# Scan decays moved from PSUM to SBUF, the freed banks given to a shared ring, pieces placed anew

## Chip, core and metric

One NeuronCore of one Trainium2 chip runs the whole program. The metric is device time of that core in microseconds (us); one execution was also taken with the hardware profiler. The engines are TensorE (PE in the profile, with its weight loads as PEld), VectorE (DVE), ScalarE (ACT), GpSimd (POOL) and SyncE (SP), which only issues transfers here.

## What is computed

x is 4 sequences of 1024 tokens with 256 channels. After a layer norm two things are made of it: a routed feed-forward stage (eight experts, one per token), and eight state-space (Mamba) layers with 512 inner channels and 16 states. The result is x + s * silu(ffn). Almost all of the time is in the eight layers:

```
xin, z = split(x @ W_in.T);  u = silu(causal_conv(xin, 4 taps) + b)
x_dbl  = u @ W_x.T  ->  dt_raw (16), B (16), C (16)
delta  = softplus(dt_raw @ W_dt.T + b_dt);  A = -exp(A_log)
h_t[c, n] = h_{t-1}[c, n] * exp(delta_t[c] * A[c, n]) + (delta_t[c] * u_t[c]) * B_t[n]
y_t[c] = sum_n h_t[c, n] * C_t[n] + u_t[c] * D[c]
x = x + (y * silu(z)) @ W_out.T
```

## The kernel before

`program` calls `experts`, then `mamba`, then `finish`. The change touches `mamba` alone and the tables of numbers that it reads.

**Units and tiles.** `mamba` works in 64 units: 8 layers times 4 sequences times 2 halves of 512 time steps (T = 512). A unit has 64 tiles (TILES = 16 states x 4 blocks of 128 channels); tile k is state n = k // 4, block j = k % 4. For each tile:
- ScalarE makes the decay exp(delta * A), 128x512 fp32 (`exponent`, L907), into `ps_d`, two banks of PSUM, two tiles ahead of the scan;
- GpSimd makes the drive, du times a row of B repeated over the partitions, both in SBUF, into one of eight buffers in SBUF (`drive`, L875); it may be up to eight tiles ahead;
- VectorE runs the recurrence over the 512 steps as one scan instruction (L1069), whose two tensor inputs are the decay in PSUM and the drive in SBUF. In the second half of a sequence (h = 1) the start value comes from `carry`, which GpSimd keeps (L861).

After the four tiles of a state, TensorE transposes the state, four matmuls for each quarter t of the time (`turn_state`, L1225), into a ring in PSUM, `ps_r`; ScalarE multiplies by C and writes `prod` in SBUF (`weigh`, L914); TensorE turns `prod` back and adds it up in `ps_y`, four banks (`turn_back`, L1232). The eight banks of PSUM are so: `ps_d` two, `ps_r` two, `ps_y` four.

**Software pipeline.** In the slots (n, t) of a unit U the engines also do pieces of other units: the end of U-1 (`gate` L1167, `out_proj` L1313, `add_x` L1173), the late half of U+1 (x and dt projections, softplus L1127 to L1137, `make_du` L1117, z), and the early half of U+2 (the marks and the running minimum that masks overflowed sequences, `mark_over` L1078/L1080, `keep_alive` L1091, `mask_x` L846 on GpSimd, `in_x`, and the convolution). Three of the four blocks are convolved on VectorE, four steps each (L1104, then L1108 three times, all in SBUF), one on TensorE (L1284). A program order written out by hand says in which slot each piece is: the tables `RING_AT`, `SILU_AT`, `EXP_AT`, `LN_AT`, `MARK_AT`, `ALIVE_AT`, `ADD_AT`, `GATE_AT`, `SKIPY_AT`, `SOFT_AT`, `CONV_AT`, `DU_AT`, `HALO_AT`, `XM_AT`. Slots from (16, 0) on mean the next unit's slot (n - 16, t). All of an engine's work runs in this order, and waits are on counting semaphores.

**The ring.** Each thing that TensorE hands to ScalarE or VectorE through `ps_r` is an item; `item_place` gives it bank (count of items so far) % 2, and `place_free` makes TensorE wait until the reader of the item two before it is done.

Of the kernel before, what the change touches and what calls it, by code (L numbers as in the profile page):

```python
# [25 lines left out]
F32 = mybir.dt.float32  # L26
# [45 lines left out]
XD = RANK + 2 * STATES  # L72
BREP = 4
DRIVE = 8
CARRY_LAG = 9
TABLE = "natural_log_exp_and_others"


RING_AT = {"CNT": (3, 0), "O0": (4, 1), "O1": (5, 3), "XD": (4, 2), "BC": (7, 3), "DT0": (6, 0), "DT1": (6, 2), "DT2": (8, 0),
           "DT3": (9, 2), "Z0": (10, 1), "Z1": (11, 3), "Z2": (14, 1), "Z3": (15, 0), "X0": (5, 0), "X1": (8, 3),  # L80
           "X2": (10, 3), "X3": (14, 2), "C3": (17, 0)}
SILU_AT, EXP_AT, LN_AT = (4, 2), [(7, 0), (10, 1)], [(8, 3), (11, 3)]
MARK_AT, ALIVE_AT, ADD_AT = [(2, 1), (2, 2)], (3, 1), [(4, 3), (6, 1)]
PE_CONV, DVE_CONV = [3], [0, 1, 2]
GATE_AT, SKIPY_AT = [(1, 1), (1, 2), (1, 2), (1, 2)], [(1, 1), (1, 3), (1, 3), (1, 3)]
SOFT_AT = [(7, 3), (8, 3), (9, 3), (10, 2), (10, 3), (11, 3), (14, 2), (14, 3)]
CONV_AT = [(5, 2), (5, 2), (6, 0), (6, 2), (9, 2), (10, 1), (12, 2), (12, 3), (15, 1), (17, 0), (17, 3), (19, 0)]
DU_AT = [(14, 3), (14, 3)]
HALO_AT, XM_AT = (3, 2), (5, 1)
CONV_ITEMS = [f"C{j}" for j in PE_CONV]  # L90
CV = CB - len(PE_CONV)
READ_AT = {name: divmod(CB * n + t + 1, CB) for name, (n, t) in RING_AT.items()}
# [509 lines left out]
def item_place(U, h, kind, name):  # L602

    i = ITEMS[kind].index(name)
    if isinstance(items_before(U, kind)[0], int):
        return (items_before(U, kind)[0] + i) % 2
    return (h * len(ITEMS["mid"]) + PRE_ALL + i) % 2


def item_ready(U, kind, name):  # L610
# [22 lines left out]

def place_free(U, kind, name):

    i = ITEMS[kind].index(name)
    if kind == "pre0" and i < 2:
        return None
    act, vec = reads(U, kind, i - 1)
    if i >= 2 and ITEMS[kind][i - 2] in VEC_ITEMS:  # L640
        return "vec", vec
    return "act", act


def mamba(nc, w_in, w_x, w_dt, w_out, w_skip, w_conv, a_log, par, xres, ident, alive_dram, bc_dram, rate_dram):

    with ExitStack() as ctx:
# [13 lines left out]
        ones_time = sb("ones_time", [1, T], BF16)  # L661
        zeros = sb("zeros", [P, 1])

        over = sb("over_mark", [P, 2, DB, T], BF16)
        alive = [sb(f"alive{h}", [P, T]) for h in range(2)]
        xm = [sb(f"xm{h}", [P, DB, T]) for h in range(2)]
        low = sb("low", [P, 2, T])
        xpad = sb("xpad", [P, CB, TAPS - 1 + T])
# [4 lines left out]
        xdbl = sb("xdbl", [P, T])  # L673
        bcT = [sb(f"bcT{h}", [P, TC, XD]) for h in range(2)]
        soft = sb("soft", [P, CB, T])
        rates = soft[:, 0, 0:LAYERS * NA]
        relu = sb("relu", [P, CB, T])
        gated = relu
# [2 lines left out]

        brep = sb("brep", [P, BREP, T])
        drive = sb("drive", [P, DRIVE, T])
        state = [sb(f"state{k}", [P, CB, T]) for k in range(2)]
        carry = sb("carry", [P, STATES, CB])
        prod = sb("prod", [P, TC, INNER])

        ps_d = ctx.enter_context(nc.psum_tensor("ps_d", [P, 2, T], F32))
        ps_r = ctx.enter_context(nc.psum_tensor("ps_r2", [P, 2, 512], F32))
        ps_y = ctx.enter_context(nc.psum_tensor("ps_y", [P, CB, T], F32))  # L690

        par_in, par_exp, par_set, par_out = sem("par_in"), sem("par_exp"), sem("par_set"), sem("par_out")
# [15 lines left out]
        def is_first(U):  # L708
            return isinstance(U, int) and U == 0
# [13 lines left out]
        def _(sp):  # L723
# [22 lines left out]
            def store_alive(U, kind, G):  # L746
                h = G % 2
                sp.wait_ge(ring_vec, item_read(U, kind, "CNT"))
                c = (G // HALVES % BATCH) * SEQ + h * T
                sp.dma_start(alive_dram[:, c:c + T], alive[h][0:1, :]).then_inc(alive_out[h], 16)  # L750

            def store_bc(U, kind, F):
                sp.wait_ge(ring_act, item_read(U, kind, "XD"))
# [81 lines left out]
        def _(pool):  # L835
# [5 lines left out]
            def mask_x(U, kind, G, h, it):  # L841
                pool.wait_ge(ring_vec, item_read(U, kind, "CNT"))
                if not (isinstance(G, int) and G < 2):

                    pool.wait_ge(ring_ready, items_before(U, kind)[0])
                nc.gpsimd.tensor_tensor(xm[h][:], xres[:, :, bass.ds((it % BATCH) * SEQ + h * T, T)],  # L846
                                        alive[h][:].unsqueeze(1).to_broadcast([P, DB, T]), ALU.mult).then_inc(xm_set, 1)

            def halo(U, kind, F, h):

# [45 lines left out]
        def _(act):  # L896
            def exponent(U, h, k):

                n, j = divmod(k, CB)
                if k in (0, CB // 2):  # L900
                    act.wait_ge(delta_set, 2 * U + k // 2 + 1)
                if not (is_first(U) and k < 2):
                    act.wait_ge(scanned, TILES * U + k - 1)
                a = j * STATES + n
                if k == 0:
                    act.wait_ge(cur_in[h], loads_of(U, h))
                nc.scalar.activation(ps_d[:, k % 2, :], delta[h][:, j, :], ACT.Exp, scale=cur[h][:, a:a + 1]).then_inc(decay_set, 1)  # L907

            def weigh(U, h, kind, item, V, n, t):

# [97 lines left out]
            def unit(U, h, it, kind):  # L1008
                for n in range(STATES):
                    for t in range(TC):  # L1010
                        k = CB * n + t + 2
                        if k < TILES:
                            exponent(U, h, k)
                        elif kind != "last":
                            exponent(U + 1, 1 - h, k - TILES)
                        if (n, t) == SILU_AT:
                            if kind != "last":
                                silu_u(U, kind, U + 1)
                            silu_z(U, h, kind)
                            nc.scalar.preload_act_table_set(TABLE)  # L1020
                        if kind != "last":
                            late(U, h, kind, U + 1, 1 - h, n, t)
                        if kind in ("first", "mid"):
                            early(U, h, kind, U + 2, n, t)
                        if n:
                            weigh(U, h, kind, ("S", n - 1, t), U, n - 1, t)
                        elif kind != "first":
                            weigh(U, h, kind, ("S", "prev", t), U - 1, STATES - 1, t)
# [13 lines left out]
            for n in range(STATES):  # L1042
                for t in range(TC):
                    early(0, 0, "pre1", 1, n, t)
            exponent(0, 0, 0)
            exponent(0, 0, 1)
            units(act, unit)
            for t in range(TC):
                weigh(UNITS, 0, "end", ("S", "prev", t), UNITS - 1, STATES - 1, t)
# [2 lines left out]
        def _(dve):  # L1052
            def scan(U, h, it, kind, n, j):
                k = CB * n + j
                dve.wait_ge(decay_set, TILES * U + k + 1)
                dve.wait_ge(drive_set, TILES * U + k + 1)
                if j == 0 and not (is_first(U) and n < 2):

                    if n >= 2:
                        dve.wait_ge(ring_ready, item_ready(U, kind, ("S", n - 2, TC - 1)))  # L1060
                    elif n == 1:
                        dve.wait_ge(ring_ready, item_ready(U, kind, ("S", "prev", TC - 1)))
                    else:
                        dve.wait_ge(ring_ready, items_before(U, kind)[0])
                    if h == 0 and n >= 2:
                        dve.wait_ge(carried, STATES * it + n - 1)
                    if h == 1:
                        dve.wait_ge(carried, STATES * it + min(STATES - 1 + n, STATES))
                nc.vector.tensor_tensor_scan(state[n % 2][:, j, :], ps_d[:, k % 2, :], drive[:, k % DRIVE, :],  # L1069
                                             carry[:, n, j:j + 1] if h == 1 else 0.0, ALU.mult, ALU.add).then_inc(scanned, 1)  # L1070

            def mark_over(U, kind, F, h, it, side):

                if kind != "pre0":
                    dve.wait_ge(ring_vec, items_before(U, kind)[1])
                xs = xres[:, :, bass.ds((it % BATCH) * SEQ + h * T, T)]
                if side == 0:
                    nc.vector.tensor_scalar(over[:, 0], xs, LIMIT, None, ALU.is_gt).then_inc(over_set, 1)  # L1078
                else:
                    nc.vector.tensor_scalar(over[:, 1], xs, -LIMIT, None, ALU.is_lt).then_inc(over_set, 1)  # L1080

            def keep_alive(U, h, kind, F, hf):

                dve.wait_ge(ring_ready, item_ready(U, kind, "CNT"))
                if not (isinstance(F, int) and F < 2):
                    dve.wait_ge(xm_set, F - 1)
                    if isinstance(F, int):
                        dve.wait_ge(alive_out[hf], 16 * (F // 2))
                    else:
                        dve.wait_ge(alive_out[hf], 8 * (F - hf))  # L1090
                nc.vector.tensor_tensor_scan(alive[hf][:], ps_r[:, item_place(U, h, kind, "CNT"), :], zeros[:, 0:1].to_broadcast([P, T]),  # L1091
                                             alive[0][:, T - 1:T] if hf == 1 else 1.0, ALU.min, ALU.max).then_inc(ring_vec, 1)

            def conv(copied, G, h, j, k):

# [436 lines left out]
```

## Time and profile before

| | us |
|---|---|
| median of 3 runs | 7806.82 |
| lowest, highest | 7770.17, 7848.79 |
| the profiled execution, its own time | 7796.76 |
| its span in the trace | 7795.0 |
| mean granted TensorE clock | 0.991 |

The span runs from the first instruction to the end of the last; busy times of the engines overlap. A number behind "idle before" in a row is the time in which that engine did nothing just before the instructions of the row, with what ended it.

### The profile page before, as it was taken

What the parts mean: (1) busy time and instruction counts of PE and PEld (TensorE: products, weight loads), DVE (VectorE), ACT (ScalarE), POOL (GpSimd) and SP (SyncE); (2) the same over time, 40 slices, a digit from 0 to 9 for tenths busy, and PEclk for the clock granted to TensorE, in tenths of its full rate; (3) what the DMA queues carried; (4) which work ended last, traced back from release to release, by engine and by line L of the source; (5) the groups of instructions that cost most, each with busy time, mean ns of one, the idle gap of its engine ahead of it and who ended that gap; (6) DMA issues with size and microseconds to landing.
All of it is one profiled execution on the core that took longest, in us unless ns stands there. A gap on an engine that the chain in (4) does not pass through costs nothing. (4 is left out here: it accounts for less than half of the span.)

```text
span 7795.0 us, 144019 instructions
## 1 busy us (share of the span) xinstructions
PE 6935.7 (89%) x39999; PEld 4781.3 (61%) x40063; DVE 6645.2 (85%) x6512; ACT 6436.9 (83%) x10314; POOL 5919.1 (76%) x4917
## 2 busy tenths in 40 slices
PE   6978999888999999999899999999998899999887
PEld 4646666666666666666666666666666666666665
DVE  3259888988988898889888988988898898889888
ACT  2248888888888888888888888888888888888887
POOL 2137888787888888888878887888888778888875
PEclk9989999999999999999999999999999999999998
DMA  4111111111111111111111111111111111111112
GB/s 160 33 40 37 39 40 47 42 38 38 42 45 43 39 39 43 46 40 40 39 46 44 40 38 42 45 42 39 39 47 42 38 39 42 45 43 39 39 38 90
DMA packets 222613, 352.40 MB, mean 45 GB/s; under 512 B 43856, under 2 KB 78448, under 8 KB 221712
## 3 DMA queue, kind: packets, MB, share of 16 engines
q1 hardware_dynamic: 218048, 332.70, 14.5%
q0 software_dynamic: 3792, 10.38, 0.4%
q8 instruction: 365, 5.98, 0.3%
q14 instruction: 408, 3.34, 0.1%
HBM read 325.00 MB, written 17.98 MB: 44 GB/s over the span
## 5 line engine op out<-in xcount | busy, mean ns | idle before, releaser
L875 POOL TENSOR_TENSOR drive<-du,brep 128x512 f32<-128x512 f32 x4096 | 5495.8, 1371 | 715.0 <-DVE du L1117 360.0
L907 ACT ACTIVATE ps_d<-delta,cur 128x512 f32<-128x512 f32 x4096 | 2844.6, 695 | 447.3 <-DVE state L1069 428.1
L914 ACT ACTIVATE prod<-ps_r,bcT 128x512 f32<-128x512 f32 x4096 | 2807.1, 685 | 240.0 <-PE ps_r L1225 235.4
L1225 PE MATMUL ps_r<-ident,state 128*128 128x128 f32 x16384 | 2552.5, 279 | 326.1 <-ACT prod L914 180.5
L1069 DVE TENSOR_TENSOR_SCAN state<-ps_d,carry,drive 128x512 f32<-128x512 f32 x2048 | 2503.2, 1264 | 308.9 <-PE ps_r L1225 274.8
L1069 DVE TENSOR_TENSOR_SCAN state<-ps_d,drive 128x512 f32<-128x512 f32 x2048 | 2390.7, 1207 | 300.8 <-PE ps_r L1225 239.6
L1232 PE MATMUL ps_y<-ident,prod 128*128 128x128 f32 x16384 | 2467.1, 275 | 25.9 <-ACT prod L914 25.9
L1232 PEld LDWEIGHTS ps_y<-ident,prod 128*128 128x128 f32 x16384 | 1928.7, 142 | 663.5 <-issue 511.7
L1225 PEld LDWEIGHTS ps_r<-ident,state 128*128 128x128 f32 x16384 | 1834.7, 141 | 773.4 <-ACT prod L914 497.3
L1273 PE MATMUL ps_r<-xm,w_inz_sb 128*128 128x512 f32 x1024 | 509.1, 620 | 89.3 <-ACT prod L914 89.3
L1265 PE MATMUL ps_r<-xm,w_inx_sb 128*128 128x512 f32 x1024 | 509.1, 621 | 25.4 <-ACT prod L914 13.9
L1313 PE MATMUL ps_r<-relu,w_out_sb 128*128 128x512 f32 x1024 | 474.2, 606 | 58.7 <-ACT prod L914 56.0
L1108 DVE SCALAR_TENSOR_TENSOR xc<-xpad,taps,xc 128x512 f32<-128x512 f32 x576 | 505.4, 877 | 4.2 <-issue 1.5
L861 POOL COPY carry<-state 128x4 f32<-128x4 f32 x512 | 226.3, 442 | 232.2 <-DVE state L1069 230.3
L1306 PE MATMUL ps_r<-xdbl,w_dt_sb 16*128 16x512 f32 x512 | 290.1, 647 | 90.2 <-DVE xres L1173 47.2
L1313 PEld LDWEIGHTS ps_r<-relu,w_out_sb 128*128 128x128 f32 x1024 | 184.7, 190 | 273.3 <-issue 217.7
L1273 PEld LDWEIGHTS ps_r<-xm,w_inz_sb 128*128 128x128 f32 x1024 | 174.4, 190 | 270.1 <-ACT prod L914 134.5
L1265 PEld LDWEIGHTS ps_r<-xm,w_inx_sb 128*128 128x128 f32 x1024 | 175.9, 191 | 196.0 <-issue 154.5
L534 ACT ACTIVATE hid<-ps_t,b_sb 128x128 f32<-128x128 f32 x312 | 84.8, 382 | 227.5 <-PE ps_t L495 227.5
L1292 PE MATMUL ps_r<-u,w_x_sb 128*48 128x512 f32 x512 | 233.7, 600 | 34.1 <-ACT u L942 34.1
L462 POOL DMA_INDIRECT ys_dram<-yb,row x39 | 37.4, 959 | 296.8 <-DVE yb L554 296.8
L1243 PE MATMUL ps_y<-u,skip 128*128 128x512 f32 x512 | 241.3, 594 | 4.6 <-DVE relu L1167 4.5
(148 smaller groups left out, 4586.5 us busy)
## 6 DMA issues: line engine op xcount, KB each, us to landing
brep<-bc_dram SPq DMA_DIRECT2D x1024, 256.0 KB, 3.2
w_sb<-w SPq DMA_DIRECT2D x8, 1024.0 KB
w_all<-w SPq DMA_DIRECT2D x8, 1024.0 KB, 11.4
xb<-xs_dram SPq DMA_DIRECT2D x39, 128.5 KB, 2.0
w_all<-x SPq DMA_DIRECT2D x4, 1024.0 KB, 9.0
w_inx_sb<-w_in SPq DMA_DIRECT2D x8, 512.0 KB, 4.0
w_inz_sb<-w_in SPq DMA_DIRECT2D x8, 512.0 KB, 4.4
w_out_sb<-w_out SPq DMA_DIRECT2D x8, 512.0 KB, 4.3
```

What stands on the lines that cost most here:

```text
L875: nc.gpsimd.tensor_tensor(drive[:, k % DRIVE, :], du[:, j, :], brep[:, n % BREP, :], ALU.mult).then_inc(drive_set, 1)
L907: nc.scalar.activation(ps_d[:, k % 2, :], delta[h][:, j, :], ACT.Exp, scale=cur[h][:, a:a + 1]).then_inc(decay_set, 1)
L914: nc.scalar.activation(prod[:, t, :], ps_r[:, item_place(U, h, kind, item), :], ACT.Copy, scale=bcT[(h + 1) % 2 if item[1] == "prev" else ...
L1069: nc.vector.tensor_tensor_scan(state[n % 2][:, j, :], ps_d[:, k % 2, :], drive[:, k % DRIVE, :], carry[:, n, j:j + 1] if h == 1 else 0.0, ...
L1108: step = nc.vector.scalar_tensor_tensor(xc[:, j, :], xpad[:, j, tap:tap + T], w, xc[:, j, :], ALU.mult, ALU.add)
L1225: last = nc.tensor.transpose(out[:, j * P:(j + 1) * P], state[n % 2][:, j, t * P:(t + 1) * P], ident[:])
L1232: last = nc.tensor.matmul(ps_y[:, j, t * P:(t + 1) * P], prod[:, t, j * P:(j + 1) * P], ident[:], start=False, stop=True, is_transpose=Tru ...
L1243: last = nc.tensor.matmul(ps_y[:, j, :], skip[:, j, :], u[:, j, :], start=True, stop=True, skip_group_check=True)
L1265: last = nc.tensor.matmul(out, w_inx_sb[:, k, j * P:(j + 1) * P], xm[h][:, k, :], start=(k == 0), stop=(k == DB - 1))
L1273: last = nc.tensor.matmul(out, w_inz_sb[:, k, j * P:(j + 1) * P], xm[hf][:, k, :], start=(k == 0), stop=(k == DB - 1))
L1306: nc.tensor.matmul(out, w_dt_sb[:, j * P:(j + 1) * P], xdbl[0:RANK, :], start=True, stop=True).then_inc(ring_ready, 1)
L1313: last = nc.tensor.matmul(out, w_out_sb[:, j, k * P:(k + 1) * P], gated[:, j, :], start=(j == 0), stop=(j == CB - 1))
```

## The change

1. The decays go to `decay`, four buffers of 128x512 in SBUF, and ScalarE is four tiles ahead of the scan in place of two (LEAD = 4). The scan then has both of its tensor inputs in SBUF.
2. The two banks of `ps_d` join the ring: `ps_r` has four banks (RING = 4), and `place_free` looks four items back.
3. To find room in SBUF, the overflow marks `over` lie in the third and fourth quarter of `soft` (so `mark_over` also waits on `delta_set`), and the two `alive` buffers become one (`keep_alive` waits for the mask before and for the store before).
4. All tables of slots have new values.

```diff
+LEAD = 4
+RING = 4
-RING_AT = {"CNT": (3, 0), "O0": (4, 1), "O1": (5, 3), "XD": (4, 2), "BC": (7, 3), "DT0": (6, 0), "DT1": (6, 2), "DT2": (8, 0),
-           "DT3": (9, 2), "Z0": (10, 1), "Z1": (11, 3), "Z2": (14, 1), "Z3": (15, 0), "X0": (5, 0), "X1": (8, 3),
-           "X2": (10, 3), "X3": (14, 2), "C3": (17, 0)}
-SILU_AT, EXP_AT, LN_AT = (4, 2), [(7, 0), (10, 1)], [(8, 3), (11, 3)]
-MARK_AT, ALIVE_AT, ADD_AT = [(2, 1), (2, 2)], (3, 1), [(4, 3), (6, 1)]
+RING_AT = {"CNT": (0, 3), "O0": (3, 3), "O1": (4, 1), "XD": (7, 3), "BC": (10, 1), "DT0": (8, 3), "DT1": (9, 2),
+           "DT2": (10, 3), "DT3": (12, 3), "Z0": (13, 1), "Z1": (13, 3), "Z2": (14, 1), "Z3": (15, 2), "X0": (2, 3),
+           "X1": (6, 0), "X2": (9, 1), "X3": (15, 1), "C3": (16, 2)}
+SILU_AT, EXP_AT, LN_AT = (4, 0), [(10, 1), (13, 1)], [(11, 2), (14, 1)]
+MARK_AT, ALIVE_AT, ADD_AT = [(0, 2), (0, 2)], (0, 3), [(4, 1), (5, 0)]
-GATE_AT, SKIPY_AT = [(1, 1), (1, 2), (1, 2), (1, 2)], [(1, 1), (1, 3), (1, 3), (1, 3)]
-SOFT_AT = [(7, 3), (8, 3), (9, 3), (10, 2), (10, 3), (11, 3), (14, 2), (14, 3)]
-CONV_AT = [(5, 2), (5, 2), (6, 0), (6, 2), (9, 2), (10, 1), (12, 2), (12, 3), (15, 1), (17, 0), (17, 3), (19, 0)]
-DU_AT = [(14, 3), (14, 3)]
-HALO_AT, XM_AT = (3, 2), (5, 1)
+GATE_AT, SKIPY_AT = [(1, 0), (1, 0), (1, 0), (1, 1)], [(1, 0), (1, 0), (1, 2), (1, 2)]
+SOFT_AT = [(11, 0), (11, 3), (12, 1), (14, 1), (14, 1), (14, 1), (14, 3), (15, 0)]
+CONV_AT = [(4, 1), (4, 3), (6, 1), (8, 3), (9, 0), (9, 1), (10, 0), (10, 3), (12, 3), (13, 0), (14, 2), (16, 1)]
+DU_AT = [(15, 0), (15, 3)]
+HALO_AT, XM_AT = (1, 0), (2, 2)
...
 def item_place(U, h, kind, name):
...
-        return (items_before(U, kind)[0] + i) % 2
-    return (h * len(ITEMS["mid"]) + PRE_ALL + i) % 2
+        return (items_before(U, kind)[0] + i) % RING
+    return (h * len(ITEMS["mid"]) + PRE_ALL + i) % RING
...
 def place_free(U, kind, name):
-    i = ITEMS[kind].index(name)
-    if kind == "pre0" and i < 2:
+    i = ITEMS[kind].index(name) - RING
+    if kind == "pre0" and i < 0:
         return None
-    act, vec = reads(U, kind, i - 1)
-    if i >= 2 and ITEMS[kind][i - 2] in VEC_ITEMS:
-        return "vec", vec
-    return "act", act
+    if i < 0:
+        before = {"pre1": "pre0", "first": "pre1", "mid": "mid", "near": "mid", "last": "near", "end": "last"}[kind]
+        assert not any(x in VEC_ITEMS for x in ITEMS[before][i:])
+        return "act", items_before(U, kind)[2] + i + 1
+    act, vec = reads(U, kind, i + 1)
+    return ("vec", vec) if ITEMS[kind][i] in VEC_ITEMS else ("act", act)
...
-        over = sb("over_mark", [P, 2, DB, T], BF16)
-        alive = [sb(f"alive{h}", [P, T]) for h in range(2)]
+        alive = sb("alive", [P, T])
...
+        over = soft[:, 2:4, :].rearrange("p a t -> p (a t)").bitcast(BF16).rearrange("p (s k t) -> p s k t", s=2, k=DB)
...
+        decay = sb("decay", [P, LEAD, T])
...
-        ps_d = ctx.enter_context(nc.psum_tensor("ps_d", [P, 2, T], F32))
-        ps_r = ctx.enter_context(nc.psum_tensor("ps_r2", [P, 2, 512], F32))
+        ps_r = ctx.enter_context(nc.psum_tensor("ps_r2", [P, RING, 512], F32))
...
             def exponent(U, h, k):
-                if not (is_first(U) and k < 2):
-                    act.wait_ge(scanned, TILES * U + k - 1)
+                if not (is_first(U) and k < LEAD):
+                    act.wait_ge(scanned, TILES * U + k + 1 - LEAD)
...
-                nc.scalar.activation(ps_d[:, k % 2, :], delta[h][:, j, :], ACT.Exp, scale=cur[h][:, a:a + 1]).then_inc(decay_set, 1)
+                nc.scalar.activation(decay[:, k % LEAD, :], delta[h][:, j, :], ACT.Exp, scale=cur[h][:, a:a + 1]).then_inc(decay_set, 1)
...
             def scan(U, h, it, kind, n, j):
-                nc.vector.tensor_tensor_scan(state[n % 2][:, j, :], ps_d[:, k % 2, :], drive[:, k % DRIVE, :],
+                nc.vector.tensor_tensor_scan(state[n % 2][:, j, :], decay[:, k % LEAD, :], drive[:, k % DRIVE, :],
                                              carry[:, n, j:j + 1] if h == 1 else 0.0, ALU.mult, ALU.add).then_inc(scanned, 1)
...
             def mark_over(U, kind, F, h, it, side):
                 if kind != "pre0":
                     dve.wait_ge(ring_vec, items_before(U, kind)[1])
+                    dve.wait_ge(delta_set, 2 if kind == "pre1" else 2 * U + 2)
...
             def keep_alive(U, h, kind, F, hf):
-                if not (isinstance(F, int) and F < 2):
-                    dve.wait_ge(xm_set, F - 1)
+                if not is_first(F):
+                    dve.wait_ge(xm_set, F)
                     if isinstance(F, int):
-                        dve.wait_ge(alive_out[hf], 16 * (F // 2))
+                        dve.wait_ge(alive_out[1 - hf], 16 * ((F + hf) // 2))
                     else:
-                        dve.wait_ge(alive_out[hf], 8 * (F - hf))
-                nc.vector.tensor_tensor_scan(alive[hf][:], ps_r[:, item_place(U, h, kind, "CNT"), :], zeros[:, 0:1].to_broadcast([P, T]),
-                                             alive[0][:, T - 1:T] if hf == 1 else 1.0, ALU.min, ALU.max).then_inc(ring_vec, 1)
+                        dve.wait_ge(alive_out[1 - hf], 8 * (F + hf))
+                nc.vector.tensor_tensor_scan(alive[:], ps_r[:, item_place(U, h, kind, "CNT"), :], zeros[:, 0:1].to_broadcast([P, T]),
+                                             alive[:, T - 1:T] if hf == 1 else 1.0, ALU.min, ALU.max).then_inc(ring_vec, 1)
```

## Rows read from the trace of the kernel before

**Rows 1.** Table of stretches, one steady and one before the units: busy us of each engine.

```profile
2100.00:2800.00 700.00, 634.09 (x3734) 436.45 (x3739) 628.35 (x595) 609.87 (x962) 568.78 (x461) 1.00 0.15 42
450.00:500.00 50.00, 35.71 (x67) 12.56 (x66) 22.93 (x26) 19.59 (x26) 2.53 (x2) 0.80 0.09 31
```

**Rows 2.** The page's costliest groups: busy us, mean ns of one, idle before and releaser.

```profile
L875 POOL TENSOR_TENSOR drive<-du,brep 128x512 f32<-128x512 f32 x4096 | 5495.8, 1371 | 715.0 <-DVE du L1117 360.0
L907 ACT ACTIVATE ps_d<-delta,cur 128x512 f32<-128x512 f32 x4096 | 2844.6, 695 | 447.3 <-DVE state L1069 428.1
L914 ACT ACTIVATE prod<-ps_r,bcT 128x512 f32<-128x512 f32 x4096 | 2807.1, 685 | 240.0 <-PE ps_r L1225 235.4
L1069 DVE TENSOR_TENSOR_SCAN state<-ps_d,carry,drive 128x512 f32<-128x512 f32 x2048 | 2503.2, 1264 | 308.9 <-PE ps_r L1225 274.8
L1069 DVE TENSOR_TENSOR_SCAN state<-ps_d,drive 128x512 f32<-128x512 f32 x2048 | 2390.7, 1207 | 300.8 <-PE ps_r L1225 239.6
```

**Rows 3.** Table of waits of the whole span: us in total, times, longest.

```profile
DVE state L1069 <- PE ps_r L1225: 514.4, 263, 9.4
PE ps_r L1225 <- ACT prod L914: 180.5, 326, 2.2
```

**Rows 4.** The scans' line: durations min/median/max, first and last start.

```profile
L1069 DVE TENSOR_TENSOR_SCAN state<-ps_d,drive x2048: 1189/1207/1226, 519.1 to 7640.6; 128x512 f32<-128x512 f32 x187
L1069 DVE TENSOR_TENSOR_SCAN state<-ps_d,carry,drive x2048: 1248/1259/1285, 632.0 to 7727.5; 128x512 f32<-128x512 f32 x187
```

**Rows 5.** Timeline, GpSimd drives beside scans: start us, us, instructions merged.

```profile
4119.25 4.97 POOL L875 TENSOR_TENSOR drive<-du,brep 128x512 f32<-128x512 f32 x4
...
4137.17 5.71 DVE L1069 TENSOR_TENSOR_SCAN state<-ps_d,drive 128x512 f32<-128x512 f32 x5
...
4117.90 8.32 DVE L1069 TENSOR_TENSOR_SCAN state<-ps_d,carry,drive 128x512 f32<-128x512 f32 x7
```

**Rows 6.** Timeline, one convolution step on VectorE between two drives on GpSimd.

```profile
4114.32 1.28 POOL L875 TENSOR_TENSOR drive<-du,brep 128x512 f32<-128x512 f32 x1
...
4115.27 0.87 DVE L1108 SCALAR_TENSOR_TENSOR xc<-xpad,taps,xc 128x512 f32<-128x512 f32 x1
...
4115.55 1.73 POOL L875 TENSOR_TENSOR drive<-du,brep 128x512 f32<-128x512 f32 x1
```

**Rows 7.** Timeline, VectorE pieces of 1024 columns beside a drive on GpSimd.

```profile
4109.45 1.27 POOL L875 TENSOR_TENSOR drive<-du,brep 128x512 f32<-128x512 f32 x1
...
4110.54 1.26 DVE L1130 TENSOR_TENSOR low<-soft,low 128x1024 f32<-128x1024 f32 x1
...
4130.71 1.21 DVE L1117 TENSOR_TENSOR du<-delta,u 128x1024 f32<-128x1024 f32 x1
...
4130.95 2.10 POOL L875 TENSOR_TENSOR drive<-du,brep 128x512 f32<-128x512 f32 x1 [6.73 <-DVE du L1117]
```

**Rows 8.** Lines with their durations over the whole span, min/median/max ns.

```profile
L875 POOL TENSOR_TENSOR drive<-du,brep x4096: 1251/1275/2301, 505.4 to 7720.6; 128x512 f32<-128x512 f32 x196
L1108 DVE SCALAR_TENSOR_TENSOR xc<-xpad,taps,xc x576: 716/755/5796, 460.0 to 7553.5; 128x512 f32<-128x512 f32 x192
L1104 DVE TENSOR_SCALAR xc<-xpad,taps x192: 514/547/1923, 459.5 to 7528.2; 128x512 f32<-128x512 f32 x192
L1134 DVE TENSOR_TENSOR low<-low,delta x128: 1191/1196/1226, 486.3 to 7631.6; 128x1024 f32<-128x1024 f32 x128
L1127 DVE TENSOR_SCALAR low<-soft x128: 660/668/1623, 483.6 to 7611.7; 128x1024 f32<-128x1024 f32 x128
L1078 DVE TENSOR_SCALAR over_mark<-xres x64: 659/661/686, 447.4 to 7432.0; 128x1024 bf16 x60, 128x1024 bf16<-128x1024 f32 x4
L846 POOL TENSOR_TENSOR xm<-xres,alive x64: 2337/2362/2379, 452.6 to 7446.5; 128x1024 f32<-128x1024 f32 x64
```

**Rows 9.** Groups by line and form, VectorE: one input in PSUM, or both in SBUF.

```profile
L1452 DVE TENSOR_TENSOR clean<-clean,valid 128x1024 f32<-128x1024 f32 x8 | 9.8, 1225 | 0.3
L1463 DVE TENSOR_TENSOR gate<-gate,ps_f 128x1024 f32<-128x1024 f32 x8 | 9.7, 1214 | 0.0
L1167 DVE TENSOR_TENSOR relu<-ps_y,zs 128x512 f32<-128x512 f32 x256 | 160.9, 667 | 5.1 <-PE ps_y L1232 5.1
```

**Rows 10.** Groups by line: TensorE's convolution, and ScalarE's silus and table loads.

```profile
L1284 PE MATMUL ps_r<-xpad,conv_w 128*128 128x512 f32 x512 | 232.0, 595 | 0.8 <-ACT xpad L920 0.8
L942 ACT ACTIVATE u<-xc 128x2048 f32<-128x2048 f32 x64 | 122.7, 1917 | 0.7
L942 ACT ACT_TABLE_LOAD x64 | 82.1, 1283 | 1.2
```

More of the change, by code:

```diff
@@ L74 @@
 DRIVE = 8
+LEAD = 4
+RING = 4
 CARRY_LAG = 9
 TABLE = "natural_log_exp_and_others"
-RING_AT = {"CNT": (3, 0), "O0": (4, 1), "O1": (5, 3), "XD": (4, 2), "BC": (7, 3), "DT0": (6, 0), "DT1": (6, 2), "DT2": (8, 0),
-           "DT3": (9, 2), "Z0": (10, 1), "Z1": (11, 3), "Z2": (14, 1), "Z3": (15, 0), "X0": (5, 0), "X1": (8, 3),
-           "X2": (10, 3), "X3": (14, 2), "C3": (17, 0)}
-SILU_AT, EXP_AT, LN_AT = (4, 2), [(7, 0), (10, 1)], [(8, 3), (11, 3)]
-MARK_AT, ALIVE_AT, ADD_AT = [(2, 1), (2, 2)], (3, 1), [(4, 3), (6, 1)]
-PE_CONV, DVE_CONV = [3], [0, 1, 2]
-GATE_AT, SKIPY_AT = [(1, 1), (1, 2), (1, 2), (1, 2)], [(1, 1), (1, 3), (1, 3), (1, 3)]
-SOFT_AT = [(7, 3), (8, 3), (9, 3), (10, 2), (10, 3), (11, 3), (14, 2), (14, 3)]
-CONV_AT = [(5, 2), (5, 2), (6, 0), (6, 2), (9, 2), (10, 1), (12, 2), (12, 3), (15, 1), (17, 0), (17, 3), (19, 0)]
-DU_AT = [(14, 3), (14, 3)]
-HALO_AT, XM_AT = (3, 2), (5, 1)
+RING_AT = {"CNT": (0, 3), "O0": (3, 3), "O1": (4, 1), "XD": (7, 3), "BC": (10, 1), "DT0": (8, 3), "DT1": (9, 2),
[3 more added lines that the diff above has]
+MARK_AT, ALIVE_AT, ADD_AT = [(0, 2), (0, 2)], (0, 3), [(4, 1), (5, 0)]
+PE_CONV, DVE_CONV = [3], [0, 1, 2]
+GATE_AT, SKIPY_AT = [(1, 0), (1, 0), (1, 0), (1, 1)], [(1, 0), (1, 0), (1, 2), (1, 2)]
+LOW_AT = [(3, 3), (8, 0)]
+SOFT_AT = [(11, 0), (11, 3), (12, 1), (14, 1), (14, 1), (14, 1), (14, 3), (15, 0)]
+CONV_AT = [(4, 1), (4, 3), (6, 1), (8, 3), (9, 0), (9, 1), (10, 0), (10, 3), (12, 3), (13, 0), (14, 2), (16, 1)]
+DU_AT = [(15, 0), (15, 3)]
+HALO_AT, XM_AT = (1, 0), (2, 2)
 CONV_ITEMS = [f"C{j}" for j in PE_CONV]
@@ L749, in store_alive @@
                 c = (G // HALVES % BATCH) * SEQ + h * T
-                sp.dma_start(alive_dram[:, c:c + T], alive[h][0:1, :]).then_inc(alive_out[h], 16)
+                sp.dma_start(alive_dram[:, c:c + T], alive[0:1, :]).then_inc(alive_out[h], 16)
             def store_bc(U, kind, F):
@@ L846, in mask_x @@
                 nc.gpsimd.tensor_tensor(xm[h][:], xres[:, :, bass.ds((it % BATCH) * SEQ + h * T, T)],
-                                        alive[h][:].unsqueeze(1).to_broadcast([P, DB, T]), ALU.mult).then_inc(xm_set, 1)
+                                        alive[:].unsqueeze(1).to_broadcast([P, DB, T]), ALU.mult).then_inc(xm_set, 1)
             def halo(U, kind, F, h):
@@ L1010, in unit @@
                     for t in range(TC):
-                        k = CB * n + t + 2
+                        k = CB * n + t + LEAD
                         if k < TILES:
@@ L1044, in _ @@
                     early(0, 0, "pre1", 1, n, t)
-            exponent(0, 0, 0)
-            exponent(0, 0, 1)
+            for k in range(LEAD):
+                exponent(0, 0, k)
             units(act, unit)
```

## The prediction

> **What bounds the kernel now.** I read first the table of stretches: in a steady 700 us TensorE is busy 634, VectorE 628, ScalarE 610 and GpSimd 569 us, at full clock [rows 1]. Four engines are within 10% of each other, so no engine alone is the bound; what each waits for must be read next. The scans run from 519.1 to 7727.5 + 1.3 = 7728.8 us [rows 4]; that is 7209.7 us for 64 units, **112.65 us for a unit**, 1.76 us for each of its 64 tiles. 519.1 us lie ahead and 7795.0 - 7728.8 = 66.2 us behind. VectorE is at work for 628/700 of a unit, 101.1 us, and idle for 11.5. The table of waits says for what: 514.4 us, 8.0 a unit, are scans that wait for TensorE's transposes, at most 9.4 us at once [rows 3], and TensorE in its turn waits 180.5 us for ScalarE to empty the ring of two banks. ScalarE sits idle for 428.1 us because decays may be made only two tiles ahead of the scans [rows 2]. These are the stalls that the change aims at: the two short queues between TensorE, ScalarE and VectorE.
>
> **What VectorE and GpSimd do to each other.** This is the view that decides, since the change alters where a scan reads. GpSimd's drive (two inputs in SBUF) takes 1.27 us as a rule but up to 2.30 [rows 8]. The timeline shows when. Beside scans four drives in a row take 4.97 us, one every (4.97 - 1.27)/3 = 1.23, and five scans 5.71, one every (5.71 - 1.22)/4 = 1.12 (1.18 with a carry, from 8.32 for seven) [rows 5]: neither feels the other. A scan has one tensor input in PSUM. Now a convolution step, whose two tensor inputs are both in SBUF: the drive ahead of it ends at 4114.32 + 1.28 = 4115.60; the step, begun at 4115.27, ends at 4116.14, 0.54 after that drive, and takes 0.87 in place of the 0.72 that it takes alone; the next drive, begun at 4115.55, ends at 4117.28, 1.14 after the step, and takes 1.73 [rows 6]. So they don't overlap at all: each does its data part only when the other is done. The same with 1024 columns: a softplus piece ends 4111.80 - 4110.72 = 1.08 after the drive that was running, and the drive that begins during a du piece ends 4133.05 - 4131.92 = 1.13 after it and takes 2.10 [rows 7]. VectorE's pieces with one input in PSUM (the gate, 667 ns in the mean [rows 9]) show no such stretch. I read it as a path into SBUF that VectorE's second SBUF input and GpSimd's reads share, held by one instruction at a time: a drive holds it for 1.13 us, a VectorE instruction of 1024 fp32 columns for 1.08, one of 512 for 0.54.
>
> The Trainium skill says this as a rule ("SBUF — State Buffer", Who interferes with whom): a VectorE instruction with two SBUF inputs contends with a GpSimd instruction that reads SBUF, and the loser is blocked for the whole instruction. It names no scan, and no row here has a long scan with two SBUF inputs; by that rule every one of the 4096 would take turns with a drive, which is my forecast.
>
> **The change, part by part.**
>
> *Decays in SBUF.* All scans now have two tensor inputs in SBUF. Their own duration should stay: two inputs in SBUF take 1225 ns and one of them in PSUM 1214, same shape [rows 9]. But what a scan holds must be bounded. It takes 1207 ns for 512 steps, as a 1024-column piece does (1196) [rows 4, 8], so it moves an element every second cycle for as long; the nearest row for its hold is that piece, 1.08 us. Above, its own start-to-start, 1.12, or 1.18 with a carry [rows 5]; below nothing, if a scan doesn't read through that path (rival one). The 57 ns that a carry adds (1264 against 1207 [rows 2]) may lie in the hold or not: half of the units have it, and I take half of it in them, 0.015 in the mean, and as much again for the hand-over. A drive: 1.13, above it its start-to-start, 1.23 [rows 5]. So a tile costs 1.08 + 0.03 + 1.13 = **2.24 us** (bounds 2.21 and 1.16 + 1.23 = 2.39), in place of 1.76, and 64 tiles cost **143.4 us** (141.4 to 153.0). Being ahead doesn't help, since both instructions have to pass for each tile.
>
> *What else passes there in a unit*: nine convolution steps of 0.54, 4.9; three first steps, alone 0.51 with some 0.17 outside the hold (0.72 - 0.54, as in the other steps), 1.0; six softplus pieces of two inputs and two du pieces, 8 x 1.08 = 8.6; two of one input, faster by half (0.66), and two marks (0.66), 4 x 0.5 = 2.0; GpSimd's mask, 2.36 - 0.14 = 2.2; eight carry copies of four columns, 0.4 together [rows 6 to 8]. Whether the one-input forms hold the path is less sure; nothing else changes if not. Sum **19.1** (17 if not).
>
> *Lead of four, ring of four.* They take away waits of VectorE, TensorE and ScalarE: 8.0 + 2.8 + 6.7 us a unit. These engines have 101 us of work or less in a unit [rows 1], which now lasts over 160, so the waits were going to be hidden by the slower tile anyway: **zero** gained. The same holds for what the decay costs ScalarE in SBUF rather than PSUM: even 0.1 us more, 6 us a unit, has 50 us of cover. The silus at (4, 0) keep ScalarE from decays for 1.92 and 1.89 us with two table loads of 1.28, 6.4 us [rows 10]; four tiles ahead are 4 x 2.24 = 9.0, so no scan waits for them; with the lead of two it would be 1.9 us a unit.
>
> The Trainium skill has a rule that speaks for the change here ("VectorE: DVE Perf Modes", the TRN2 errata): VectorE's fixed cost is 120 cycles from PSUM against 58 in SBUF, by which 4096 scans would be an estimated 260 us cheaper. The rows of one shape don't show it (1214 against 1225), and with a path that is full a shorter fixed part buys nothing.
>
> *Pieces placed anew.* Their count is the same, so the sum above stays; the question is where the path is idle because both engines wait. Three places at the start of a unit: (a) du comes at (15, 0) and (15, 3), where before both pieces came at (14, 3). GpSimd may make only drives 0 and 1 of the next unit until scan 63 and du are done; scans 61 to 63 use the path meanwhile, nothing lost; bound 2 x 1.13. (b) GpSimd waits at (1, 0) for the last convolution step and TensorE's item C3 (for the halo) with everything queued behind it, drives 5 on; it has five drives done by then. (c) The gates are at (1, 0), behind scan 4, and wait for all of the unit before to be turned back: TensorE needs four quarters of about 1.2 us, C3 at 232.0/64 = 3.6 [rows 10], the count and four more turns, some 12 us; VectorE needs for four scans, a step, two marks and `alive` about 4 x 2.24 + 0.5 + 1.3 + 1.25 = 12. They come out even, so I take 1.5 us a unit for all three, from 0 up to the 8.0 that such waits cost today. The added waits of the marks on `delta_set` and of `alive` on the mask at (2, 2) of the unit before and on its store are for work done most of a unit earlier: nothing. SP's loads of B rows wait for the drives as before and have more time.
>
> *Sum*: 143.4 + 19.1 + 1.5 = **164 us a unit**; 64 x 164 = 10,496, + 519.1 + 66.2 = 11,081 us of span, + 1.8 to the execution's own time = 11,083. The median of the runs shown is 10 above that execution, so **11,090**.
>
> **TensorE's clock** is a side question. At 634 of 700 us busy it is granted 1.00; in 450 to 500 us, 35.7 of 50 busy, it is 0.80, part of the time at 1.2 in place of 2.4 GHz [rows 1]. TensorE's 102 us in 164 are less still, so I expect a granted mean below 0.99. Slow stretches stay under the 63 us of cover, apart from the chain at the start of a unit, which is in the upper bound.
>
> **Rivals.** (1) *A scan doesn't take the shared path, even with both inputs in SBUF* (a rate of one element in two cycles could be served by VectorE's own input alone). For it: no row shows such a scan beside a drive. Against: two kinds of VectorE instruction, of two tensor inputs, are both serialised. Then the lead and the ring do what they are for: VectorE's 101.1 us of work and from 0 to all of its waits of 11.5, 64 x 101.1 + 587 = 7,060 to 7,800, likeliest 7,450. This is the case of the other side; it decides as soon as a tile's two holds together fall under 1.76 us, that is a scan's hold under 0.6. Chance 0.06. (2) *Half a hold*: the scan holds the path as an instruction of 512 columns does, 0.54. A tile then costs 1.67 on the path, 106.9 + 19.1 = 126 us a unit, and with 5 of waits 131: 8,970. Chance 0.05. (3) *The path and the chain together*: TensorE at 1.2 GHz for much of the time makes its 102 us nearly twice that, scans wait for it again, at over 180 us a unit: above 12,100. Chance 0.04. (4) *The change doesn't do what it says*: the four banks could wait for a reader that isn't the item four back. `place_free` waits for exactly that count, also over a unit's edge; and it would be hidden. Chance inside the forecast's.
>
> **How the numbers follow.** Forecast 0.85, (1) 0.06, (2) 0.05, (3) 0.04. The forecast's bounds: low, 141.4 + 17 + 0 = 158.4 a unit, 10,725; high, 153.0 + 19.1 + 8 = 180.1, 12,120. Most of (3) lies outside, and the top of the forecast needs all three upper bounds at once; below 10,725 I leave 2% for a hold somewhat shorter than the nearest row. So 10,560 to 11,800. Within 1% is about what a measurement of this kernel (7770 to 7849) can tell from no change: faster 0.05, same 0.02, slower 0.93.
>
> **What would show it.** In the changed profile: drives at about 2.2 us in place of 1.27, scans at up to 2.3, in strict turns, the end of each 1.08 to 1.13 after the end of the other; GpSimd and VectorE both near full, TensorE and ScalarE near 60%; the wait of scans for TensorE nearly gone. If drives stay at 1.27 beside scans, rival one is right and my number is wrong by half; if a scan ends 0.54 after a drive, rival two; if both engines show idle time at the start of each unit, my 1.5 us is too small.

## The result, and the profile after

The changed kernel takes 10,788.5 us (median of 4 runs, 10,784.3 to 10,789.3), beside 7799.2 for the kernel before: 1.382 times as long, 95% interval 1.375 to 1.390. The forecast was 11,090, range 10,560 to 11,800.

The page of the changed kernel, busy time by engine and the granted clock in 40 slices:

```profile
span 10785.8 us, 144296 instructions
...
PE 7845.5 (73%) x40000; PEld 5739.1 (53%) x40063; DVE 10257.6 (95%) x6512; ACT 6623.7 (61%) x10314; POOL 8937.8 (83%) x4917
...
PEclk9978888888888888888888888888888888888887
```

Four engines stood within 10% of each other in a steady stretch before [rows 1]; now there is one that is always busy, VectorE, with GpSimd next. These of the page's costliest groups (busy us, mean ns of one, idle time before and what ended it) answer to [rows 2]:

```profile
L880 POOL TENSOR_TENSOR drive<-du,brep 128x512 f32<-128x512 f32 x4096 | 8247.8, 2041 | 1234.9 <-DVE du L1123 768.6
L912 ACT ACTIVATE decay<-delta,cur 128x512 f32<-128x512 f32 x4096 | 2953.1, 721 | 3710.3 <-DVE state L1074 3705.1
...
L1074 DVE TENSOR_TENSOR_SCAN state<-decay,carry,drive 128x512 f32<-128x512 f32 x2048 | 4037.7, 2020 | 1.8 <-POOL carry L866 1.3
L1074 DVE TENSOR_TENSOR_SCAN state<-decay,drive 128x512 f32<-128x512 f32 x2048 | 3892.9, 1949 | 2.9 <-PE ps_r L1231 2.2
...
L919 ACT ACTIVATE prod<-ps_r,bcT 128x512 f32<-128x512 f32 x4096 | 2758.1, 673 | 14.5 <-PE ps_r L1231 12.7
```

A drive takes 2041 ns in the mean where it took 1371, a scan 1949 and 2020 where it took 1207 and 1264. The idle time ahead of the scans, 609.7 us before (308.9 + 300.8), is down to 4.7: the stalls that the deeper queues were to remove are gone, and the time is 2989 us longer all the same. It has gone into the instructions themselves. Their line by durations, min/median/max, beside [rows 4 and 8]:

```profile
L1074 DVE TENSOR_TENSOR_SCAN state<-decay,drive x2048: 1190/2224/3296, 517.8 to 10579.1; 128x512 f32<-128x512 f32 x187
L1074 DVE TENSOR_TENSOR_SCAN state<-decay,carry,drive x2048: 1251/2226/3307, 673.5 to 10717.5; 128x512 f32<-128x512 f32 x187
...
L880 POOL TENSOR_TENSOR drive<-du,brep x4096: 1258/2184/2271, 505.3 to 10711.9; 128x512 f32<-128x512 f32 x196
```

The shortest scan, 1190 ns, is as short as before (1189): from SBUF a scan is no slower by itself. The median is longer by 1.02 us, nearly the length of a drive. The timeline shows the turns, first four scans of VectorE, then four drives of GpSimd, about 1.1 us earlier (start us, us from the first start to the last end, instructions merged):

```profile
5020.92 8.67 DVE L1074 TENSOR_TENSOR_SCAN state<-decay,drive 128x512 f32<-128x512 f32 x4
```

```profile
5019.83 8.68 POOL L880 TENSOR_TENSOR drive<-du,brep 128x512 f32<-128x512 f32 x4
```

With 2.23 for one, that is a scan every (8.67 - 2.23)/3 = **2.15 us**, in step with one drive; in [rows 5] it was 1.12 for scans and 1.23 for drives, neither minding the other. Where GpSimd has nothing to do, at the end of the unit while it waits 9.4 us for du, the same instructions are short at once. First VectorE, then GpSimd:

```profile
5139.89 1.22 DVE L1074 TENSOR_TENSOR_SCAN state<-decay,drive 128x512 f32<-128x512 f32 x1
5141.02 1.20 DVE L1140 TENSOR_TENSOR low<-low,delta 128x1024 f32<-128x1024 f32 x1
5142.14 1.22 DVE L1074 TENSOR_TENSOR_SCAN state<-decay,drive 128x512 f32<-128x512 f32 x1
```

```profile
5145.77 2.03 POOL L880 TENSOR_TENSOR drive<-du,brep 128x512 f32<-128x512 f32 x1 [9.39 <-DVE du L1123]
```

The scans run from 517.8 to 10,718.8 us, (10,718.8 - 517.8)/64 = **159.4 us a unit**, where it was 112.65.

### The profile page after: what moved, and what is told of

It is laid out like the page before. It is cut to its first block and busy times, and to the rows that moved or that the text cites. A ratio compares the mean times of both kernels' runs of the same rounds, so it can differ in the third digit from the quotient of the medians.

```text
span 10785.8 us, 144296 instructions
## 1 busy us (share of the span) xinstructions
PE 7845.5 (73%) x40000; PEld 5739.1 (53%) x40063; DVE 10257.6 (95%) x6512; ACT 6623.7 (61%) x10314; POOL 8937.8 (83%) x4917
## 5 line engine op out<-in xcount | busy, mean ns | idle before, releaser
L880 POOL TENSOR_TENSOR drive<-du,brep 128x512 f32<-128x512 f32 x4096 | 8247.8, 2041 | 1234.9 <-DVE du L1123 768.6
L912 ACT ACTIVATE decay<-delta,cur 128x512 f32<-128x512 f32 x4096 | 2953.1, 721 | 3710.3 <-DVE state L1074 3705.1
L1231 PE MATMUL ps_r<-ident,state 128*128 128x128 f32 x16384 | 3003.6, 315 | 2117.7 <-DVE state L1074 1487.2
L1074 DVE TENSOR_TENSOR_SCAN state<-decay,carry,drive 128x512 f32<-128x512 f32 x2048 | 4037.7, 2020 | 1.8 <-POOL carry L866 1.3
L1074 DVE TENSOR_TENSOR_SCAN state<-decay,drive 128x512 f32<-128x512 f32 x2048 | 3892.9, 1949 | 2.9 <-PE ps_r L1231 2.2
L1231 PEld LDWEIGHTS ps_r<-ident,state 128*128 128x128 f32 x16384 | 2273.1, 164 | 2438.0 <-ACT prod L919 1139.8
L1238 PE MATMUL ps_y<-ident,prod 128*128 128x128 f32 x16384 | 2929.2, 312 | 13.4 <-ACT prod L919 13.4
L1238 PEld LDWEIGHTS ps_y<-ident,prod 128*128 128x128 f32 x16384 | 2361.6, 165 | 719.1 <-issue 525.5
L1114 DVE SCALAR_TENSOR_TENSOR xc<-xpad,taps,xc 128x512 f32<-128x512 f32 x576 | 811.6, 1409 | 0.6
L866 POOL COPY carry<-state 128x4 f32<-128x4 f32 x512 | 441.2, 862 | 116.2 <-DVE state L1074 116.2
```

The lines of the kernel that those rows point to most:

```text
L866: nc.gpsimd.tensor_copy(carry[:, n, :], state[n % 2][:, :, T - 1]).then_inc(carried, 1)
L880: nc.gpsimd.tensor_tensor(drive[:, k % DRIVE, :], du[:, j, :], brep[:, n % BREP, :], ALU.mult).then_inc(drive_set, 1)
L912: nc.scalar.activation(decay[:, k % LEAD, :], delta[h][:, j, :], ACT.Exp, scale=cur[h][:, a:a + 1]).then_inc(decay_set, 1)
L1074: nc.vector.tensor_tensor_scan(state[n % 2][:, j, :], decay[:, k % LEAD, :], drive[:, k % DRIVE, :], carry[:, n, j:j + 1] if h == 1 else 0 ...
L1114: step = nc.vector.scalar_tensor_tensor(xc[:, j, :], xpad[:, j, tap:tap + T], w, xc[:, j, :], ALU.mult, ALU.add)
L1231: last = nc.tensor.transpose(out[:, j * P:(j + 1) * P], state[n % 2][:, j, t * P:(t + 1) * P], ident[:])
```

## The experiments

Eight kernels, in two groups, each group on one chip with the kernel before beside it (7774.9 us in the first, 7814.9 in the second).

**1. The operand alone.** The tables of slots are those of the kernel before; LEAD and RING are 2; the decays stay in SBUF. Against the changed kernel:

```diff
-LEAD = 4
-RING = 4
+LEAD = 2
+RING = 2
...
-RING_AT = {"CNT": (0, 3), ...
+RING_AT = {"CNT": (3, 0), ...
...
```

> The slots, the ring of two and the lead of two of the kernel before; only the decays lie in SBUF, two buffers (with the changed kernel's room for marks and alive, which makes the place). Shared-path theory: where the scan reads is the whole cause, so scans and drives take turns at 2.15 us a tile as in the changed kernel; unit 157 to 164 us, time 10,650 to 11,100. Rival (new slots, ring or aliased buffers made the kernel slow): about 7,800, and drives stay at 1.27 us. In between only if both matter.

Measured 10,924 us, 1.406 times the kernel before (1.403 to 1.408). The scans:

```profile
L1073 DVE TENSOR_TENSOR_SCAN state<-decay,drive x2048: 1190/2223/2297, 520.6 to 10717.6; 128x512 f32<-128x512 f32 x187
L1073 DVE TENSOR_TENSOR_SCAN state<-decay,carry,drive x2048: 1248/2223/2437, 678.1 to 10854.2; 128x512 f32<-128x512 f32 x187
```

The same median to a nanosecond or three with the old slots, ring and lead: where the scan reads is enough for the whole slowdown. All else in the change together is worth about 136 us (10,924 against 10,788, measured with a kernel before of 7774.9 and of 7799.2), and on the right side.

**2. Its control.** The same kernel with the decays in two banks of PSUM:

```diff
-        decay = sb("decay", [P, LEAD, T])
+        decay = ctx.enter_context(nc.psum_tensor("ps_d", [P, LEAD, T], F32))
```

> The same kernel with the decays back in two banks of PSUM: that is the kernel before with the marks in soft and one alive buffer. Shared-path theory: the room-making costs nothing, 7,750 to 7,870. Rival (the added waits on delta_set and on the mask cost time): above 7,900.

Measured 7781.9, ratio 1.0007 (0.9998 to 1.0017), a unit of 112.7 us. So the marks that share the room of `soft`, the one `alive` buffer and their added waits cost nothing. This kernel and the one above differ by that one line, and by 3142 us.

**3 and 4. A quarter and a half of the tiles.** Against the first experiment, decays of block 0, and of blocks 0 and 2, stay in SBUF, the others lie in PSUM:

```diff
+SBUF_J = (0,)        # in the other (0, 2)
         decay = sb("decay", [P, LEAD, T])
+        ps_d = ctx.enter_context(nc.psum_tensor("ps_d", [P, LEAD, T], F32))
+        place_d = lambda k: (decay if k % CB in SBUF_J else ps_d)[:, k % LEAD, :]
```

> As the control, but the decays of block j = 0, one tile in four, lie in SBUF. Shared path with VectorE in order: each such scan stands up to 1.03 us until a drive is done (2.23 against 1.20 us), 16 x 1.03 = 16.5 us a unit on top of VectorE's 100.4 of work, the old waits of 11 partly absorbed: unit 117 to 126, time 8,070 to 8,650. Capacity alone as the limit (1.07 x 64 + 1.08 x 16 + 19 = 105 us, less than the 112.65 now): no change, 7,800. No sharing: 7,800.

> As before with blocks 0 and 2, half of the tiles, in SBUF. In-order waiting: 100.4 + 32 x 1.03 = 133.4 us of VectorE a unit, plus 0 to 6 of waits: 133 to 140, time 9,120 to 9,550. Capacity alone (1.07 x 64 + 1.08 x 32 + 19 = 122 us): 8,400. Straight line between none and all: 136 us, 9,290.

Measured 8496 us (ratio 1.094, 1.092 to 1.095) and 9232 us (1.188, 1.186 to 1.190). So none, a quarter, a half and all cost 0, 714, 1450 and 3142 us over the control. That only the path's capacity counts is refuted: with a quarter the path has 105 us of work in a unit of 112.65, and yet the kernel is 9% slower. The totals are in the expected ranges, but their make-up is not what I reckoned. The groups of the quarter:

```profile
L1076 DVE TENSOR_TENSOR_SCAN state<-ps_d,carry,drive 128x512 f32<-128x512 f32 x1536 | 1894.5, 1260 | 20.5 <-ACT ps_d L914 17.8
L1076 DVE TENSOR_TENSOR_SCAN state<-ps_d,drive 128x512 f32<-128x512 f32 x1536 | 1806.1, 1201 | 29.1 <-ACT ps_d L914 28.2
L1076 DVE TENSOR_TENSOR_SCAN state<-decay,carry,drive 128x512 f32<-128x512 f32 x512 | 958.8, 1873 | 345.6 <-PE ps_r L1233 340.9
L1076 DVE TENSOR_TENSOR_SCAN state<-decay,drive 128x512 f32<-128x512 f32 x512 | 798.4, 1559 | 291.7 <-PE ps_r L1233 280.9
```

In one program and one trace, scans with the decay in PSUM take 1201 and 1260 ns and those with it in SBUF 1559 and 1873. In the mean that is 1.716 us, 0.49 more than the 1.231 beside them and 0.48 more than the 1.236 of the control, not 1.03: a drive is not always in the way when such a scan begins (half of those without a carry take under 1266 ns). And the old waits were not absorbed: scans still wait 621.8 us for TensorE (514.4 before [rows 3]). VectorE is busy for 110.4 us (overlaps counted once) in a unit of (8425.6 - 520.8)/64 = 123.5; in the control it is 100.4 in 112.7. So 16 scans add 7.7 us, other pieces of VectorE about 2.2, and idle time 1. I had reckoned with 16.5 us for the scans and with fewer waits: the ranges were met by luck, since the two errors cancelled.

**5 and 6. GpSimd that only writes.** In the kernel before (as a control) and in the changed one, GpSimd writes zeros in place of du times B (the products are left out; nothing waits on `pool_waited`):

```diff
-                        nc.gpsimd.tensor_tensor(drive[:, k % DRIVE, :], du[:, j, :], brep[:, n % BREP, :],
-                                                ALU.mult).then_inc(drive_set, 1)
+                        pool.sem_inc(pool_waited, 1)
+                        nc.gpsimd.memset(drive[:, k % DRIVE, :], 0.0).then_inc(drive_set, 1)
```

> The kernel before, in which GpSimd only writes zeros to the drive buffers in place of du times B (the products are left out, so the state stays 0). All waits of the drive stay. It is the control for the next kernel. VectorE's convolution and softplus pieces no longer find GpSimd in the way, 2 to 4 us a unit less; the waits on TensorE and ScalarE stay. 7,500 to 7,750.

> The changed kernel, GpSimd writing zeros in the same way (the same part left out). Shared-path theory, only GpSimd's reads count: scans at 1.2 us with both inputs in SBUF; then lead and ring of four show what they are worth without the contention: VectorE some 97 us of work a unit plus 0 to 5 of waits, 6,850 to 7,250, clearly below the control. Rival (any instruction of GpSimd shuts a two-input scan out, also one that only writes): scan plus 0.4 us, 125 us a unit or more, above 8,500. Rival (a scan from SBUF is slow by itself): scans near 2.2 us, about 10,000.

Measured 7688.2 us (0.984, 0.980 to 0.987) and 7441.9 us (0.952, 0.949 to 0.955). The scans of the second, both inputs in SBUF:

```profile
L1074 DVE TENSOR_TENSOR_SCAN state<-decay,drive x2048: 1187/1201/3320, 513.4 to 7295.4; 128x512 f32<-128x512 f32 x187
L1074 DVE TENSOR_TENSOR_SCAN state<-decay,carry,drive x2048: 1248/1264/1548, 619.5 to 7380.4; 128x512 f32<-128x512 f32 x187
```

Median 1201 and 1264, as from PSUM in [rows 4]: both rivals fall, and it is GpSimd's reads that shut a scan out. GpSimd isn't held up either: its writes take 524 ns in the median and 514 at the shortest. Nor is ScalarE's writing of the decays into SBUF the cause, since it goes on here. The one-input softplus pieces are less clear: they take 952 ns in the mean, against 669 in experiment 5 where GpSimd only writes too, and one that began at 3169.84 us and took 1.54 ran beside three such writes, so they may meet GpSimd's writes also.

The pair also prices the rest of the change where scans and drives don't meet: 7441.9/7688.2 = 0.968, **3.2% faster**. The first of the two was as expected; the second is slower than the 6,850 to 7,250 that I had expected, 5.7 to 10.9% below the control. VectorE's work is 98.1 us a unit in both; its idle time falls from 13.0 to 9.2 only. The table of waits of the second shows what remains:

```profile
DVE state L1074 <- PE ps_r L1231: 297.6, 234, 5.1
...
DVE xc L1110 <- ACT u L947: 152.6, 62, 4.3
```

Waits for TensorE are halved (574.7 in the control), and the first convolution step, now right behind the silus, waits 2.4 us a unit for ScalarE to have read `xc`. TensorE is busy for 643.7 and ScalarE for 626.1 of a steady 700 us there; at those shares TensorE's work is 643.7/700 x 107.3 = 98.7 us a unit, which no depth of a queue takes away.

**7. One read in place of two.** The changed kernel, with GpSimd copying du (no product):

```diff
-                        nc.gpsimd.tensor_tensor(drive[:, k % DRIVE, :], du[:, j, :], brep[:, n % BREP, :],
-                                                ALU.mult).then_inc(drive_set, 1)
+                        pool.sem_inc(pool_waited, 1)
+                        nc.gpsimd.tensor_copy(drive[:, k % DRIVE, :], du[:, j, :]).then_inc(drive_set, 1)
```

> The changed kernel, in which GpSimd copies du to the drive buffer (the product with B is left out): one SBUF input in place of two. Path held for the time that the data take: if one input of 512 columns needs about half of the product's 1.07 us, a tile costs 1.08 + 0.5 = 1.6 us, a unit 118 to 128 us, 8,150 to 8,800. If each turn costs the same whatever is read: 10,790.

Measured 8233.8 us (1.053, 1.049 to 1.058). The timeline, VectorE and then GpSimd:

```profile
4017.89 10.46 DVE L1074 TENSOR_TENSOR_SCAN state<-decay,carry,drive 128x512 f32<-128x512 f32 x7
```

```profile
4016.84 11.92 POOL L881 COPY drive<-du 128x512 f32<-128x512 f32 x8
```

With 1.56 for one scan, a turn lasts (10.46 - 1.56)/6 = 1.48 us, 0.67 less than with two reads. With 1.08 for the scan, the copy holds the path 0.40 us and the product 1.07. So a turn has no fixed price. The hold goes by GpSimd's instruction: the shortest copy takes 602 ns and the shortest product 1258, each 0.19 or 0.20 us more than its hold. Whether the number of inputs or the operation makes that length, this run doesn't separate.

**8. Lead of two in the changed kernel.** `LEAD = 2`, ring and slots kept:

> The changed kernel with the lead back at two (two decay buffers in SBUF, ring of four and slots kept). The lead is worth nothing in the full path except at the silus, which keep ScalarE for 6.4 us against 2 x 2.15 of lead, 2.1 us a unit at most: 10,790 to 10,930. Rival (ScalarE's decays are on the path): more than 11,000.

Measured 10,804.7 us, ratio 1.382 (1.378 to 1.387), the same as the changed kernel's. The waits of scans for decays come back just where they were expected, 64 of them, one in each unit:

```profile
DVE state L1074 <- ACT decay L912: 94.9, 64, 4.1
```

That is 1.5 us a unit of waiting, of which the unit (159.7 against 159.4) shows 0.3: while VectorE waits, GpSimd has the path to itself, and VectorE's later pieces are shorter (the convolution steps 1330 ns in the mean against 1409).

Not run: the new slots with the decays in PSUM. They were laid out for a ring of four, and eight banks don't hold more than two beside two of decays and four of `ps_y`; what they would do with a ring of two isn't shown. Nor was a mixture run with the new slots. It is unlikely to pay: 16 tiles in SBUF cost 10.8 us a unit (123.5 against 112.7), while lead, ring and slots together gave 111.1 - 107.3 = 3.8 in experiments 5 and 6. Of the kernels here that compute everything, none is faster than the kernel before.

## Why the prediction was right

**The mechanism** was read rightly from [rows 6 and 7], where convolution and softplus pieces took turns with drives; that scans would do the same was the part that no row showed. Experiment 1 and its control show it with one line and experiments 3 and 4 within one trace; experiment 6 shows that it is GpSimd's reading.

**The tile, 2.24 us:** 2.15 measured. This is the term that was mis-sized: 64 x 0.09 = 5.8 us of a unit forecast at 164 and measured at 159.4; the other terms were 1.2 too small together. The scan's hold was 1.08 as the 1024-column piece gave. The drive's was 1.07, not 1.13. Here is one scan of VectorE, and the drive that began during it:

```profile
5060.47 2.22 DVE L1074 TENSOR_TENSOR_SCAN state<-decay,drive 128x512 f32<-128x512 f32 x1
```

```profile
5061.57 2.19 POOL L880 TENSOR_TENSOR drive<-du,brep 128x512 f32<-128x512 f32 x1
```

The drive ends 5063.76 - 5062.69 = 1.07 after the scan, as 2.15 - 1.08 says. Why it was 1.13 or 1.14 behind the pieces of [rows 6, 7] isn't shown. The carry's 57 ns lie outside the scan's hold: 2224 and 2226 ns are the medians without and with a carry. My added 0.03 was for nothing; the low bound, 2.21, was already too high. With it and the 19.1 a unit would have been 160.5 at least. That 159.4 still lies above the forecast's low end of 158.4 comes from the 17 us there for what else passes, which was too low in its turn.

**What else passes, 19.1 us, and 1.5 of idle path:** taken together 159.4 - 64 x 2.15 = 21.8 us against 20.6; how they divide wasn't measured. Pieces with one input belong there, which I had left open. The second mark takes 1749 ns in the median, where it took 661:

```profile
L1086 DVE TENSOR_SCALAR soft<-xres x64: 684/1749/1753, 447.1 to 10278.9; 128x1024 bf16 x60, 128x1024 bf16<-128x1024 f32 x4
...
L1173 DVE TENSOR_TENSOR relu<-ps_y,zs x256: 656/674/692, 689.0 to 10725.7; 128x512 f32<-128x512 f32 x128
```

The gate, with an input in PSUM, is never stretched (692 at most). Both are as the Trainium skill has it ("SBUF — State Buffer", Who interferes with whom). So are the turns of whole instructions, here and in experiment 7. Its rule on fixed costs ("VectorE: DVE Perf Modes", the TRN2 errata), by which scans from SBUF would be cheaper, isn't borne out for the scan: the shortest are 1190 ns from SBUF and 1189 from PSUM.

**Lead and ring at zero:** right in the sum, though not exactly: lead, ring and slots took VectorE's idle time from 10.1 us a unit (experiment 1, 161.5 with 151.4 busy) to 2.5, and the unit fell by only 2.1; that a full path hid the rest is how I read it. **The silus** behave as reckoned: 1.5 us of wait a unit with a lead of two, where I had said 1.9. **The start of a unit** shows no large stall: VectorE's idle time is those 2.5 us a unit in all, 1.3 of it the first convolution step waiting for ScalarE and 0.9 `alive` waiting for the count. **The waits for du** grew from 360.0 to 768.6 us for GpSimd, as du comes later in the new slots. No cost of them shows: in the stretch above VectorE goes on without a gap in that time, and its instructions are short.

**TensorE's clock** fell to a granted mean of 0.86, 0.87 in a steady stretch, from 0.991: with 510 of 700 us busy it spends part of the time at 1.2 GHz. Its busy time is 116 us a unit, where it was 102, so it is busy for 73% and not for the 60% forecast. Hardly a scan waits for it (4.7 us of idle time before all scans), so it costs nothing here.

**The rivals.** *Not on the shared path* would need drives of 1.27 us beside scans; they are 2.18. *Half a hold* would end a scan 0.54 after a drive; in the timeline the fourth scan ends at 5020.92 + 8.67 = 5029.59, 1.08 after the fourth drive (5019.83 + 8.68 = 5028.51). *Path and chain together* would show waits of scans for TensorE; there are 2.7 us. The border that the prediction gives for rival one, a scan's hold under 0.6 us, leaves out the 19.1 us of other pieces. With them the lead and the ring have something to win only below (112.65 - 19.1)/64 - 1.13 = 0.33.

## What to carry to other kernels

Before an operand moves from PSUM to SBUF, count the SBUF inputs of the instruction that reads it: a second one on VectorE puts that instruction in turns with GpSimd's instructions that read SBUF (products and copies here), each for its full data time, however many buffers lie between them. Look in the trace for any two-input piece that runs beside a GpSimd instruction; the distance from the end of one to the end of the other is the price of the turn, and it carried over from a softplus piece to a scan within a few hundredths of a microsecond. Removing stalls is worth at most their idle time, here 3.2% where scans and drives didn't meet, so a longer instruction on the busiest engine must be priced first.

## What the runs showed that I had not expected

A small share of such instructions already costs almost in proportion: a quarter of the tiles, 9.4%, although the path then has idle time, since VectorE works in order and stands behind each drive that is running. From a half to all the price rises, 1692 us for the second half against 1450 for the first. And a carry copy of four columns takes a whole turn's wait, 1112 ns in the median where it took 208, yet costs the path hardly anything. After such a copy, from 5018.74 to 5019.86 us, the next scan takes only 1.19 us, with no drive ahead of it. The copies' durations:

```profile
L866 POOL COPY carry<-state x512: 177/1112/1178, 529.6 to 10591.1; 128x4 f32<-128x4 f32 x171
```
